# Loading the rows of a batch four batches ahead instead of two, in the first two attentions of a decoder layer

## What is computed

```
x = layernorm(x + causal self-attention(x))          # 16 heads of 32, projections with a rank 16 addition, output projection
x = LN(x + self-attention(x))                         # 16 heads of 32, biases, gain and shift
x = layernorm(LN(...  x + attention(x, context) ... + relu feed forward))
x = layernorm(x + quantized feed forward(x))
```

## Time and profile before

| what | before |
|---|---|
| median of three runs | 3351.85 us (3346.13 to 3355.16) |
| span of the profiled execution | 3352.8 us (the page gives no time of this execution beside the span) |
| TensorE busy | 3122.7 us, 93% |
| VectorE busy | 2591.0 us, 77% |
| mean granted TensorE clock | 0.976 |

### The profile page before, as it was taken

The page is one execution under the profiler, slowest core; times in us unless marked ns, Lnnn a source line. Parts: engine busy times, 40 slices in busy tenths (PEclk is TensorE's granted clock), DMA queues, the critical chain, the costliest instruction groups (busy, mean ns, idle before and its releaser), DMA issues.

```text
span 3352.8 us, 88599 instructions
## 1 busy us (share of the span) xinstructions
PE 3122.7 (93%) x35500; PEld 2438.7 (73%) x35500; DVE 2591.0 (77%) x4691; ACT 2018.2 (60%) x4586; POOL 1227.7 (37%) x1128
## 2 busy tenths in 40 slices
PE   6998999999999968999999999999979999999996
PEld 4888888878889846777777777777765656565562
DVE  5777788878889757888888888888855666666666
ACT  2665556656677636777777777777763544434342
POOL 0444431126665643344444443434113212222222
PEclk9999999999999988999999999999989999999998
DMA  3566654436554545656556545555342121121212
GB/s 101 161 192 208 193 167 142 147 118 189 173 165 136 162 113 123 140 132 138 133 123 138 135 124 139 128 135 113 87 173 76 45 53 44 50 54 50 55 38 48
DMA packets 445189, 405.71 MB, mean 121 GB/s; under 512 B 270471, under 2 KB 352523, under 8 KB 443630
## 3 DMA queue, kind: packets, MB, share of 16 engines
q1 hardware_dynamic: 444526, 399.78, 44.5%
q10 hardware_dynamic: 256, 0.26, 0.0%
HBM read 239.72 MB, written 109.52 MB: 104 GB/s over the span
## 4 chain that ended last, share of the span: by engine, by line
PE 59%; DMA 13%; DVE 12%; SPq 6%; ACT 5%; issue 3%; POOL 2%; ACTq 0%; POOLq 0%; DVEq 0%
PE at_ps L752 26%; PE at_ps L876 5%; PE at_ps L896 5%; PE at_ps L839 4%; PE at_ps L1404 4%; PE at_ps L1418 3%; DMA causal_spill<-at_proj 3%; PE at_ps L1429 3%; PE at_ps L1383 3%; DMA self_spill<-at_proj 2%; DVE at_mx_cross L964 2%; PE at_ps L781 2%; DMA at_o_raw<-at_values 2%; PE at_ps L851 2%; SPq L708 1%
## 5 line engine op out<-in xcount | busy, mean ns | idle before, releaser
L971 DVE TENSOR_TENSOR at_p<-at_ps,at_p 125x448 f16<-125x448 f32 (+1 forms) x1280 | 779.6, 617 | 167.5 <-ACT at_ps L924 158.6
L923 ACT ACTIVATE at_p<-at_ps 125x448 f16<-125x448 f32 (+1 forms) x1280 | 698.8, 546 | 292.8 <-PE at_ps L876 254.2
L924 ACT ACTIVATE at_ps<-at_ps 125x448 f32<-125x448 f32 (+1 forms) x1280 | 699.4, 546 | 0.0
L964 DVE TENSOR_REDUCE at_mx_cross<-at_ps 128x1 f32<-128x750 f32 x512 | 477.2, 932 | 41.1 <-PE at_ps L839 38.3
L1044 POOL TENSOR_TENSOR at_o_sum<-at_o_raw 128x256 f32<-128x256 f32 x192 | 121.3, 632 | 930.6 <-ACT at_o_raw L930 930.4
L876 PE MATMUL at_ps<-at_stacks 97*112 97x224 f16 (+2 forms) x1792 | 324.6, 257 | 23.2 <-DMA at_stacks<-at_mrow 19.2
L896 PE MATMUL at_ps<-at_values,at_p 112*128 112x33 f16 (+3 forms) x7168 | 317.0, 185 | 12.1 <-ACT at_o_raw L930 6.7
L916 ACT ACTIVATE at_proj<-at_ps 128x448 f16<-128x448 f32 (+2 forms) x320 | 155.1, 485 | 273.7 <-PE at_ps L752 273.2
L1383 PE MATMUL at_ps<-at_xt,at_early 128*128 128x256 f16 x1792 | 303.2, 276 | 7.8 <-ACT at_w_first L1453 4.9
L1452 ACT ACTIVATE at_masks<-at_ps,at_b_cols 128x256 f32<-128x256 f32 x224 | 107.2, 479 | 336.1 <-PE at_ps L1383 336.0
L967 DVE TENSOR_REDUCE at_mx<-at_ps 128x2 f32<-128x448 f32 x512 | 304.4, 610 | 5.7 <-PE at_ps L851 4.0
(11 more groups left out here) (203 smaller groups left out, 6775.6 us busy)
## 6 DMA issues: line engine op xcount, KB each, us to landing
at_x_res<-x SPq DMA_DIRECT2D x124, 256.0 KB, 3.1
cross_spill<-at_proj SPq DMA_DIRECT2D x64, 487.0 KB, 3.1
at_x_rows<-x SPq DMA_DIRECT2D x92, 256.0 KB, 4.5
at_prep<-bit SPq DMA_DIRECT2D x32, 512.0 KB, 4.6
at_early<-ctx SPq DMA_DIRECT2D x32, 512.0 KB, 5.1
at_stacks<-cross_spill SPq DMA_DIRECT2D x64, 243.5 KB, 3.7
causal_spill<-at_proj SPq DMA_DIRECT2D x64, 224.0 KB, 2.0
at_stacks<-causal_spill SPq DMA_DIRECT2D x128, 112.0 KB, 2.3
```

The costliest lines, as they stand in the source:

```text
L923: act.activation(mem.p_hi[0:self.KC, n % 4, :], scores, ACT.Exp, scale=EXP_SCALE)
L924: act.activation(scores, scores, ACT.Exp, scale=EXP_SCALE).then_inc(self.exp_done, 1)
L964: dve.tensor_reduce(self.mx[:, at, t, h:h + 1], mem.ps_qk[:, :, 0:self.KT // 2], AX.XY, ALU.max).then_inc(self.max_done, 1)
L971: dve.tensor_tensor(mem.p_lo[0:self.KC, n % 4, :], mem.ps_st[0:self.KC, self.st_bank(b, g, n), 0:2 * T], mem.p_hi[0:self.KC, n % 4, :], AL ...
```

## The change

The `load` tokens of the two stages move from step 0 to the beginning of step 3, just behind the step in which `x1` frees the place, and load the batch four ahead instead of two ahead. Batches 2 and 3, which no step would then load, are loaded in the start-up: batch 2 between the first and the second unit's projections, batch 3 ahead of the first two `row` transfers. The number of transfers, their sizes and all other jobs stay.

```diff
 ORDERS = {
-    "causal": (("S1 E1 M0 M1 row S2 qka qkb S3 spill V0 residual stack M2 V1 v0a M3 E0 V2 v0b load S0 V3",
+    "causal": (("S1 E1 M0 M1 row S2 qka qkb S3 spill V0 residual stack M2 V1 v0a M3 E0 V2 v0b S0 V3",
                  "E1 S1 row M0 S2 store qka M1 qkb v0a S3 V0 v0b V1 E0 M2 spill ot0 stack S0 V2 ot1 M3 V3",
                  "E1 S1 S2 x0 M0 V0 qka S3 V1 qkb M1 spill S0 E0 y0a y0b x1 M2 M3 V2 v0a v0b stack y1a y1b row V3",
-                 "M0 norm E1 S1 qka M1 S2 qkb V0 V1 M2 row E0 S3 M3 S0 v0a v0b V2 spill apply V3 stack"),
+                 "M0 norm load E1 S1 qka M1 S2 qkb V0 V1 M2 row E0 S3 M3 S0 v0a v0b V2 spill apply V3 stack"),
                (5, 3, 2, 1)),
-    "self": (("M0 S1 residual load S2 E1 qka M1 S3 qkb V0 spill V1 E0 M2 M3 row S0 V2 V3 v0a v0b stack",
+    "self": (("M0 S1 residual S2 E1 qka M1 S3 qkb V0 spill V1 E0 M2 M3 row S0 V2 V3 v0a v0b stack",
                  "M0 norm row M1 S1 S2 S3 qka E1 qkb v0a V0 M2 spill M3 V1 E0 v0b V2 V3 stack apply S0",
                  "x0 S1 S2 M0 E1 qka qkb V0 S3 V1 M1 E0 v0a v0b spill x1 stack V2 V3 M2 M3 S0 row",
-                 "S1 store qka E1 M0 S2 M1 V0 qkb spill V1 M2 E0 S3 v0a v0b M3 S0 V2 row V3 stack"),
+                 "S1 store load qka E1 M0 S2 M1 V0 qkb spill V1 M2 E0 S3 v0a v0b M3 S0 V2 row V3 stack"),
                (5, 3, 2, 1)),
...
                 elif kind in ("load", "loadc"):
-                    at = resolve(b + (3 if layer.cross else 2))
+                    at = resolve(b + (3 if layer.cross else 4))
...
             yield from causal.inputs(0)
             yield from loads(1)
             yield from causal.unit(0)
+            yield from loads(2)
             yield from causal.unit(1)
             work = causal.inputs(1)
             for u in range(2, causal.JOBS_AHEAD):
                 work += list(causal.unit(u))
             maxima = [m for u in range(causal.MAX_AHEAD) for m in causal.maxima(u)]
             yield from spread(work, maxima)
+            yield from loads(3)
             for g in range(causal.ROW_AHEAD):
                 yield causal, "row", 0, g, 0
```

## The result

The changed kernel takes 3336.36 us (3325.17 to 3340.34, 6 runs) against 3352.07 us (6 runs of the kernel before beside it): a ratio of 0.9944, interval 0.9927 to 0.9961. The medians differ by 15.7 us, and the ratio stands for 18.8 us, with an interval of 13 to 24. The forecast was 24 us.

What follows compares the result with a forecast made beforehand. TensorE, busy 93% of the span, was taken as the bound, so transfers matter only where it waits. 9.4 + 3.4 + 1.5 + 10.3 + 5 - 2 - 3.3 = 24.3 us gave a median of 3328 us, range 3308 to 3347.

Steps and rivals of the forecast that it cites:

- the likeliest case: Whole kernel: the forecast itself, a time of 3315 to 3340 us, chance 0.58.
- -3.4: Causal stage, transfers behind the removed load: spill and row go out earlier, shortening seven waits for rows, -3.4 us.
- the first term: Causal stage, removed load: ten TensorE waits for x_rows vanish with the load four batches ahead, -9.4 us.
- The big weight loads: Causal stage: the row behind 3 MB of second-stage weights has 512 KB less in front, -1.5 us.
- the term of -10.3: Self stage: the spill of step 0 gains a net 1.0 us per batch, shortening waits for its stack, -10.3 us.
- the term of +2: Self stage, start of step 1: a few new waits for the stack of step 3, +2 us.
- the clock term: Self stage: shorter waits keep TensorE's granted clock higher, so matmuls take less time, -5 us.
- Rival (c): Self stage: the spill of step 3 lands after 6.1 us, its stack is late, kernel slower at 3367 us; chance 0.06.
- Rival (b): Self stage: all stack waits go and the clock stays up, 48 us gained, about 3304 us; chance 0.12.
- Rival (a): Self stage gives nothing: the spill of step 3 loses what that of step 0 gains, about 3343 us; chance 0.2.
- Rival (d): Whole kernel: nothing changes, as another engine fills in where TensorE waited; chance 0.04.
- Start: Start-up: loads of batches 2 and 3 delay a spill and the first row of maxima, +3.3 us.

Runs made afterwards that it cites:

- small_self_load: Kernel before, with the self stage's loads from its fourth batch on reading 8 of 512 columns, issues kept: 3330.78 us, ratio 0.9921.
- self_load_behind_spill: Changed kernel with the self stage's load moved to step 1, right behind that step's spill, three batches ahead: 3317.57 us, ratio 0.9897.
- self_only: Kernel before, with the load moved in the self stage alone, causal stage and start-up unchanged: 3343.01 us, ratio 0.9968.
- three_ahead_again: Second profile of the kernel before with loads at their old places, three batches ahead instead of two; that kernel took 3350.32 us, ratio 0.9993.

## Why the prediction was right, and where its reasons were not

The direction, the range and the likeliest case held: 3336 us lies in the forecast's own 3315 to 3340, with two thirds of the 24 us. Of the two large parts of the sum, that of the causal stage had about the right size by a wrong division, and that of the self stage was nearly twice too large: its queue behaved about as said, its waits did not.

**Causal stage.** Predicted -14.3 us over three terms (-9.4, -3.4, -1.5); measured, by the mean of seven profiles with the load in its new place (521.2) and four with the old code (532.8), -11.6 us, and -9.1 for the two profiles of the changed kernel alone. The waits themselves went as the first term said: no wait for `x_rows` is left, all of TensorE's waits in this stage fell from 25.5 to 16.2 us on average, and the waits for rows of maxima stayed (11.5 us in four profiles of the old code, 12.2 in seven of the new). What is wrong is the split. The first term took the lead alone to be worth the whole 9.4 us, because the window of 211 to 249 us less its waits is TensorE's busy time. That arithmetic says what the time was spent on, not what takes the place of a wait. In the batches of which this window is one it nearly holds: lead alone wins 1.1 us a batch. But over the stage it wins 2 us, since 3.4 come back in the batch with the big weight loads, and neither the first batch nor the late ones win much. The other half of the edit, the transfer and its issue taken out from in front of the spill of step 0 and put into the queue's idle time between two rows, then adds 9.6 us: 2.6 in the first batch, 1.7 in the next five, 3.4 at the weight loads and 1.8 behind them. I had priced it at 3.4 us, and expected it as fewer waits for rows. So the sum was nearly right while its terms were not, which is in part luck. The division into 2 and 9.6 us holds for this order of the two halves; the place without the lead was not run, nor the old place with four batches of lead instead of three. The load between two rows cost nothing that shows, as said. From the rows of batch 3 to those of batch 8 a batch lasts 36.7 us on average in the two profiles after and 38.0 in the two before, where 36.3 was predicted.

**The big weight loads**, -1.5: not seen. That batch lasts 46.9 us in the old code and 46.8 with the new place. In the first pair a wait of 5.89 us and one of 1.33 became 5.40 and 3.40.

**Self stage**, -10.3 and -5 for the clock, +2 for new waits, together -13.3: measured -7.1 by the means above, and this is where the sum went furthest wrong. The net of what the queue gains held: from stack to stack it takes 11.3 us on average in the five profiles of the old order and 9.9 in the four of the new one, 1.4 us less, of which 1.0 is the earlier issue and 0.4 the landing; and the stack of step 3 follows its spill after 4.0 us instead of 3.6. That is 1.4 given and 0.4 taken, where I had 2.2 and 1.2. But the waits of TensorE did not follow. From 50 to 1150 us those for the stack of step 0, at the start of step 2, fell from 17.2 to 13.4 us (means of five and of four profiles), and those for the stack of step 3, at the start of step 1, grew from 0.4 to 4.9. So the term of -10.3 gave -3.8, and the term of +2 gave +4.5: the 1.4 us of slack of the earlier trace rows did not cover a spill that lands 0.4 us later on average, since single ones take 1 to 2 us longer. With those for the stack of step 1 the sum is 20.7 us in the old order and 20.8 in the new, now in 13 to 17 waits instead of 10 to 12. What got shorter is the matmul time: 464.0 us on average in the new order and 469.1 in the old, for the same 6271 matmuls, at a granted clock of 0.973 instead of 0.961. That is 5.1 of the 7.1 us, as much as the clock term said; all waits of TensorE in the stage went from 27.0 to 25.0. The clock term was to follow from shorter waits, and why it came without a smaller sum of waits stays open.

One reading behind the sizes was wrong. I took 1.0 us for 512 KB from two spills, one behind the residual and the load alone and one behind 768 KB of preparation besides. But a write of preparation stands in front of the first one too (`w`, 256 KB). The queue of the kernel before in front of the two spills:

```profile
1001.38 0.43 SPq L264 DMA_DIRECT2D w<-at_prep  x1
...
1003.83 0.38 SPq L701 DMA_DIRECT2D self_spill<-at_proj  x1
```

```profile
966.72 0.44 SPq L252 DMA_DIRECT2D at_prep<-bit  x1
967.20 0.47 SPq L264 DMA_DIRECT2D w<-at_prep  x1
...
970.03 0.38 SPq L701 DMA_DIRECT2D self_spill<-at_proj  x1
```

They differ by the read of 512 KB, so the 1.7 us between 6.1 and 4.4 belong to 512 KB and not to 768. The second error was to add issue and data. With the data alone taken away, the issue kept, the stretch is shorter by 1.4 us (small_self_load), the same as with both taken away; in the three pairs of steps behind the preparation it is 2.0 us in either case. I read this as issue and data overlapping while the queue has transfers in front; no run separates it further.

**Rival (c)**, slower, needed a landing of 5 us and more for the spill of step 3. From that spill to its stack it takes 4.0 us on average, and single ones reached 5.5; the waits at the start of step 1 that it names did appear, 2 to 8 a profile, but with 4.9 us in all on average and not 17. They are one of the signs by which I had said I would be wrong. **Rival (b)**, 48 us and 3304, is what further moves reach, and not this change: with load and residual behind spills it is 3305.8 us. The load in front of the spill of step 3 is a part of the difference, as self_load_behind_spill shows. **Rival (a)** would have given 3343 and the self stage unchanged. Its reasoning fits the stack waits, whose sum did not fall; against it stand self_only, faster by 0.32% (0.19 to 0.46), and the stage's means, of which the lowest of the old order (493.5) lies just above the highest of the new one (492.9). **Rival (d)**, nothing changes, is not borne out by this change; lead without place is what comes near it, 0.9993.

**Start.** Predicted +3.3, measured +2.2 by the means of two profiles each (102.5 and 100.3), and +1.8 by those of all five profiles with the load of batch 3 in front of the rows and all eight without; the row's wait is 1.8 us longer (5.83 and 5.68 against 4.02 and 3.87). I had taken 3.

**The rest**, which nothing was predicted for, is 6.5 us shorter in the two profiles after than in the two before, but it is as short in other kernels that leave it alone, with either order (2215.4 in three_ahead_again, whose causal and self code keep the old places). It is not the change's doing as far as these runs show. Causal stage, self stage and start together give 9.1 + 7.1 - 2.2 = 14.0 us with the changed kernel's own two profiles for the causal stage and the start, and 11.6 + 7.1 - 1.8 = 16.9 with all profiles; the medians differ by 15.7, and the interval of the ratio is 13 to 24.

The Trainium skill ("DMA: Bandwidth & Descriptors", Specifications) would make 512 KB cost 1.5 us as an estimate from its 358 GB/s for a core; the measured 1.4 to 2.0 us agree with that better than my 1.0. Its statement that descriptors are taken in the order of a ring (same page, Queues, rings and completion order) agrees with the start: with the load in front the row is awaited 1.8 us longer, and with the load behind it about as long as in the kernel before (3.95 us and 4.02).

## What to carry to other kernels

A wait's length says what could be won at most, not what will be: when the waiting engine is let go, look at what it meets next from the same queue. Here 10.4 us of waits were taken away by lead alone and 8.2 came back at other transfers of that queue, nearly half of them in the one batch with the big weight loads, while the five batches ahead of it kept three quarters of the gain. Together with the move to where the queue stood idle, all of it was kept. A bulk transfer belongs behind a small one that somebody waits for, not in front of it. Where one code varies by several microseconds in a stage between executions, cut the span into stages, take several profiles of either side, and compare the same batches in each: a window fixed in time holds other batches in a faster kernel.

## What was not expected of the hardware

A transfer of 512 KB in front of a spill costs 1.4 us from stack to stack, whether its two issues (1.0 us there) are taken out with it or stay; I had added the two. And a self stage with the same queue takes from 493.5 to 504.3 us in five profiles, with 466.0 to 475.1 us of matmul time: in the first three of them (493.7, 497.4 and 504.3 us) 8.0 of the 10.6 us between the ends are matmul time, at a granted clock of 0.965, 0.962 and 0.946.
